# New opening orders, down-weight units moved to tiles 7, 8, 9 and 11, and 16 unread TensorE products

## The reference, cut to what matters

```python
xn = layernorm(x)                          # over the last axis
# FFN: NF4 weights, 4-bit codes with one absmax per 64 elements
Wg, Wu, Wd = dequant_nf4(gate), dequant_nf4(up), dequant_nf4(down)   # (1792,512) (1792,512) (512,1792)
ffn = (silu(xn @ Wg.T) * (xn @ Wu.T)) @ Wd.T
# S4: a 512-tap kernel K from the state matrices, a causal convolution along the last axis
s4 = irfft(rfft(xn, 1024) * rfft(K, 1024))[..., :512] + D * xn
```

## Time and profile before

| what | value |
|---|---|
| median of the runs | 471.67 us |
| the profiled execution's own time | 471.57 us |
| its span, first to last instruction | 469.7 us |
| PE (TensorE matmul) busy | 440.0 us |
| DVE busy | 396.7 us |
| ACT busy | 280.8 us |
| POOL busy | 209.1 us |
| mean granted TensorE clock | 0.993 |

### The profile page before, as it was taken

The page is one execution under the profiler, slowest core; times in us unless marked ns, Lnnn a source line. Parts: engine busy times, 40 slices in busy tenths (PEclk is TensorE's granted clock), DMA queues, the critical chain, the costliest instruction groups (busy, mean ns, idle before and its releaser), DMA issues.

```text
span 469.7 us, 7270 instructions
## 1 busy us (share of the span) xinstructions
PE 440.0 (94%) x2556; PEld 250.5 (53%) x2556; DVE 396.7 (84%) x629; ACT 280.8 (60%) x472; POOL 209.1 (45%) x180
## 2 busy tenths in 40 slices
PE   0789799999898699999999999999999999999997
PEld 0554344444343244444444444456544688888886
DVE  5966877988997979898897777969999799999993
ACT  7748737576787595687776767956232543545340
POOL 2672597364858685466655655957400000000000
PEclk9999999999999799999999999999999999999999
DMA  8461547111322454242512243347694021001101
GB/s 290 118 232 69 99 93 164 43 50 64 126 89 68 166 200 138 66 158 68 181 45 67 56 104 90 89 138 248 192 342 157 1 91 45 25 22 46 46 30 62
DMA packets 34168, 51.41 MB, mean 109 GB/s; under 512 B 13076, under 2 KB 14164, under 8 KB 33364
## 3 DMA queue, kind: packets, MB, share of 16 engines
q1 hardware_dynamic: 34132, 50.95, 35.1%
HBM read 38.03 MB, written 10.81 MB: 104 GB/s over the span
## 4 chain that ended last, share of the span: by engine, by line
PE 66%; DVE 12%; POOL 9%; issue 7%; ACT 4%; DMA 1%; SPq 0%; POOLq 0%; DVEq 0%; ACTq 0%
PE bank L2290 29%; PE bank L2417 21%; PE bank L2367 8%; PE bank L2357 6%; POOL work L885 3%; PE bank L2134 3%; ACT work L977 2%; POOL w L898 2%; DVE work L1350 1%; DVE h L1424 1%; DMA h<-in_x 1%; DVE work L1354 1%; DVE h L1539 1%; DVE h L1440 1%; POOL wd L898 1%
## 5 line engine op out<-in xcount | busy, mean ns | idle before, releaser
L977 ACT ACTIVATE work<-work 128x512 f32<-128x512 f32 (+1 forms) x234 | 130.2, 623 | 17.4 <-POOL work L885 11.4
L885 POOL TENSOR_SCALAR work<-work 128x512 f32<-128x512 int32 x39 | 85.1, 2182 | 69.5 <-DVE work L1350 56.6
L2290 PE MATMUL bank<-h 128*128 128x512 f16 x360 | 81.6, 379 | 0.5 <-DVE h L1411 0.4
L2134 PE MATMUL bank<-xT,w 128*128 128x512 f16 (+1 forms) x312 | 67.2, 374 | 4.4 <-DVE xT L1591 2.5
L2290 PEld LDWEIGHTS bank<-h 128*128 128x128 f16 x360 | 34.9, 98 | 43.8 <-issue 1.2
L2417 PE MATMUL bank<-wd,work 128*128 128x256 f16 x504 | 56.2, 273 | 0.0
L2290 PE MATMUL bank<-xT,w 128*128 128x512 f16 x240 | 55.4, 379 | 0.0
L2417 PEld LDWEIGHTS bank<-wd,work 128*128 128x128 f16 (+1 forms) x504 | 49.3, 98 | 6.0
L2134 PEld LDWEIGHTS bank<-xT,w 128*128 128x128 f16 x312 | 31.4, 101 | 37.5 <-DVE w L1364 3.1
L898 POOL TENSOR_SCALAR w<-work,sc 128x512 f16<-128x512 f32 x21 | 40.3, 1921 | 21.9 <-DVE work L1354 21.3
L1290 ACT ACTIVATE work<-h 128x896 f16<-128x896 f32 x30 | 27.9, 942 | 28.5 <-DVE h L2042 18.3
(11 more groups left out here) (196 smaller groups left out, 661.9 us busy)
## 6 DMA issues: line engine op xcount, KB each, us to landing
moved<-h SPq DMA_DIRECT2D x6, 1024.0 KB, 5.1
h<-moved SPq DMA_DIRECT2D x4, 1536.0 KB, 15.3
h<-in_x SPq DMA_DIRECT2D x8, 512.0 KB, 4.6
xT<-in_x SPq DMA_DIRECT2D x16, 256.0 KB, 3.6
out<-xT SPq DMA_DIRECT2D x15, 256.0 KB, 2.1
work<-in_q_gate SPq DMA_DIRECT2D x14, 256.0 KB, 2.8
work<-in_q_up SPq DMA_DIRECT2D x14, 256.0 KB, 3.1
work<-in_am_gate SPq DMA_DIRECT2D x28, 128.0 KB, 3.0
```

The lines of the kernel that those rows point to most:

```text
L885: pool.tensor_scalar(chain_room(u, "r"), qs[:, u % 2, :], RIGHT_FROM, RIGHT_FROM, ALU.max, ALU.subtract).then_inc(first_done, 1)
L977: nc.scalar.activation(room, qs[:, u % 2, :] if j == 0 else room, KNEE, scale=scale, bias=bias, alpha=below).then_inc(knee_done, 1)
L2134: mm = nc.tensor.matmul(out_b, weights(k)[:, unit, wl, f, :], xT[:, TPC * c + first:TPC * c + last, xl, f, :], start=(i == 0), stop=(i == ...
L2290: mm = nc.tensor.matmul(out_b, weight(wl, f), token(xl, f), start=(n == 0 and i in (1, 5)), stop=(n == 5), skip_group_check=i not in (1, 5))
```

## The change

- `EARLY_IN` goes from tiles 5, 6, 9, 12 to tiles 7, 8, 9, 11: the four down units that are made early stand between the up and the gate unit of these tiles.
- PE: ten products of the identity's bits (128x256 f16, into bank 1, unread) before the first transpose group, six more behind the fourth; `turn(7)` moves ahead of the up product of n = 1, which is no longer cut in two.
- POOL: `rstd(3)` (17 instructions) is removed; `first_pass` 4, 7 and 8 move ahead of the norms that they followed.
- DVE: `rstd(3)` in twelve steps is added; the whole list of the opening is reordered, with units 7 and 8 made before and among the token sums; the four `token_whole` of side 1 move from tile 3 into the opening. In `items` the order is WHOLE, SCALED with the unit's own `up_sums`, `weight_lo(u - 1)`; WHOLE waits for `wlo_done >= u - 2`.
- ACT: the opening is reordered; `chain(7)` and `chain(8)` come before the silus that they followed.
- SP: the absmax load of place 8 goes ahead of two small loads and of the DMA transposes of groups 12 to 15.

```diff
@@ -119,7 +119,7 @@
 
 
 
-EARLY_IN = (5, 6, 9, 12)
+EARLY_IN = (7, 8, 9, 11)
 EARLY = len(EARLY_IN)
 SEQ = list(range(9))
 for k in range(3, NM - 1):
...
@@ -490,7 +490,6 @@
         mv_done = sem("mv_done")
         acc_done = sem("acc_done")
         rs_step = sem("rs_step")
-        rs_next = sem("rs_next")
         xn_done = sem("xn_done")
...
         TURNED = 8
-        RSTD, RSTD_NEXT = 12, 17
+        RSTD = 12
...
                 turn(t)
             absmax_of(7)
             codes_of(8)
+            absmax_of(8)
             sp.dma_start(lstep, log_step.to_broadcast([P, 1])).then_inc(step_ld, 16)
             sp.dma_start(d_col, d_skip.to_broadcast([P, 1])).then_inc(d_ld, 16)
...
             for place in range(8, UNITS - 3):
                 codes_of(place + 1)
-                absmax_of(place)
+                if place > 8:
+                    absmax_of(place)
...
@@ -739,51 +740,10 @@
             pool.affine_select(out=ident[:], in_=ident[:], compare_op=ALU.not_equal, fill=1.0, base=0,
                                pattern=[[-1, P]], channel_multiplier=1).then_inc(id_done, 1)
 
-            def rstd(c):
-
...
                 c = t // TPC
-                if c < 3:
-                    pool.wait_ge(rs_step, RSTD * (c + 1))
-                else:
-                    pool.wait_ge(rs_next, RSTD_NEXT)
+                pool.wait_ge(rs_step, RSTD * (c + 1))
...
@@ -911,22 +871,21 @@
                 norm(t)
             first_pass(2)
             first_pass(3)
+            first_pass(4)
             for t in range(TPC, 2 * TPC):
                 norm(t)
-            first_pass(4)
             first_pass(5)
             for i in range(14):
                 v_step(i)
             first_pass(6)
             for t in range(2 * TPC, 3 * TPC):
                 norm(t)
-            rstd(3)
+            first_pass(7)
             for t in range(3 * TPC, NT):
                 norm(t)
-            first_pass(7)
+            first_pass(8)
             for i in range(EXP_STEPS):
                 exp_step(i)
-            first_pass(8)
...
@@ -1141,59 +1100,60 @@
             chain(1, 0, 5)
             norm(0)
             chain(1, 5, 6)
-            chain(2, 0, 1)
             x_hi(0)
             weight_hi(0)
             x_hi(1)
-            chain(2, 1, 2)
+            chain(2, 0, 1)
             x_hi(2)
             x_hi(3)
+            chain(2, 1, 2)
             weight_hi(1)
             chain(2, 2, 6)
             chain(3, 0, 2)
             weight_hi(2)
-            chain(3, 2, 6)
+            chain(3, 2, 4)
             x_hi(4)
+            chain(3, 4, 6)
+            silu(0)
+            chain(4, 0, 1)
+            weight_hi(3)
             x_hi(5)
-            weight_hi(3)
+            x_hi(6)
             act.wait_ge(b_mm, 1)
             nc.scalar.activation(yv[:, 0:2], bank[3][:, 0:2], ACT.Copy).then_inc(b_cp, 1)
-            x_hi(6)
             x_hi(7)
-            chain(4, 0, 3)
-            silu(0)
-            chain(4, 3, 6)
-            chain(5, 0, 3)
+            chain(4, 1, 6)
             h_hi(0)
             silu(1)
             weight_hi(4)
-            chain(5, 3, 6)
+            chain(5, 0, 6)
             h_hi(1)
+            silu(2)
             x_hi(8)
             weight_hi(5)
             x_hi(9)
             x_hi(10)
             x_hi(11)
-            silu(2)
+            silu(3)
             chain(6, 0, 6)
-            silu(3)
             silu(4)
             h_hi(4)
+            silu(5)
+            chain(7, 0, 6)
             x_hi(12)
             x_hi(13)
             x_hi(14)
             x_hi(15)
-            chain(7, 0, 6)
-            silu(5)
             silu(6)
+            chain(8, 0, 6)
             silu(7)
             silu(8)
             silu(9)
-            items(ACT_AT[7], ACT_AT[7] + 3)
+            weight_hi(6)
+            gate_copy(6)
             token_hi(0, 0)
             token_hi(0, 2)
             silu(10)
-            items(ACT_AT[7] + 3, ACT_AT[8])
             token_hi(0, 1)
             token_hi(0, 3)
...
-                    if u >= 2:
-
-                        dve.wait_ge(wlo_done, u - 1 if u < 4 or u in CHAINED else u)
+                    if u >= 3:
+                        dve.wait_ge(wlo_done, u - 2)
...
                     if u in CHAINED:
-                        i = (3, 2, 4)[i]
+                        i = (3, 4, 2)[i]
                     if i != 2:
                         step(u, i if i < 2 else i - 1)
                     elif u > 0:
                         weight_lo(u - 1)
-                        before = SEQ[u - 1]
-                        if before < GU and before % 2 == 1 and before // 2 in BLOCKED:
-                            up_sums(before // 2, u - 1)
+                    if i == 4 and SEQ[u] < GU and SEQ[u] % 2 == 1:
+                        up_sums(SEQ[u] // 2, u)
...
                     dve.wait_ge(xt_ld[c - 2], 16 * TPC)
+                elif s == 1 and i == 2:
+                    dve.wait_ge(xp_done, NT - POOL_NORMS)
                 elif s == 1 and i == 0:
-                    dve.wait_ge(xlo_done, NT)
+                    dve.wait_ge(xt_ld[1], 16 * TPC)
...
             step(0, SCALED)
+            step(1, WHOLE)
+            scales(7)
+            scales(8)
+            x_lo(0)
+            weight_lo(0)
+            x_lo(1)
+            step(1, SCALED)
+            x_lo(2)
+            x_lo(3)
+            weight_lo(1)
             stats(5)
             stats(6)
-            scales(7)
             stats(7)
-            scales(8)
             moments(4, 8)
-            step(1, WHOLE)
             rstd(1, 0)
             rstd(1, 1)
             rstd(1, 2)
-            x_lo(0)
+            scales(9)
             rstd(1, 3)
-            weight_lo(0)
             rstd(1, 4)
-            x_lo(1)
             rstd(1, 5)
-            step(1, SCALED)
+            step(2, WHOLE)
             rstd(1, 6)
             rstd(1, 7)
-            x_lo(2)
             rstd(1, 8)
-            x_lo(3)
+            step(2, SCALED)
             rstd(1, 9)
             rstd(1, 10)
-            weight_lo(1)
             rstd(1, 11)
-            scales(9)
-            step(2, WHOLE)
-            scales(10)
-            step(2, SCALED)
-            scales(11)
             weight_lo(2)
             stats(8)
+            x_lo(4)
+            scales(10)
             step(3, WHOLE)
+            scales(11)
+            step(3, SCALED)
+            h_mul(0)
             scales(12)
-            step(3, SCALED)
-            x_lo(4)
+            weight_lo(3)
             x_lo(5)
-            weight_lo(3)
+            x_lo(6)
             stats(9)
-            x_lo(6)
             x_lo(7)
...
             rstd(2, 2)
-            h_lo(0)
+            step(4, WHOLE)
             rstd(2, 3)
-            step(4, WHOLE)
             rstd(2, 4)
             rstd(2, 5)
             step(4, SCALED)
             rstd(2, 6)
             rstd(2, 7)
             rstd(2, 8)
-            h_mul(1)
+            h_lo(0)
...
             rstd(2, 11)
+            h_mul(1)
             weight_lo(4)
+            step(5, WHOLE)
+            step(5, SCALED)
             h_lo(1)
-            step(5, WHOLE)
+            stats(12)
             x_lo(8)
-            step(5, SCALED)
...
-            stats(12)
+            stats(13)
             weight_lo(5)
             x_lo(9)
-            stats(13)
             x_lo(10)
+            x_lo(11)
+            h_mul(2)
             stats(14)
-            x_lo(11)
             stats(15)
             moments(12, 16)
-            h_mul(2)
+            rstd(3, 0)
+            rstd(3, 1)
+            rstd(3, 2)
             h_mul(3)
+            rstd(3, 3)
+            rstd(3, 4)
+            rstd(3, 5)
             step(6, WHOLE)
+            rstd(3, 6)
+            rstd(3, 7)
+            rstd(3, 8)
             step(6, SCALED)
+            rstd(3, 9)
+            rstd(3, 10)
+            rstd(3, 11)
+            token_whole(0, 1)
             h_mul(4)
-            token_whole(0, 1)
+            token_whole(0, 3)
             h_lo(4)
-            token_whole(0, 3)
+            h_mul(5)
+            step(7, WHOLE)
+            step(7, SCALED)
             for t in range(12, 16):
                 x_lo(t)
-            h_mul(5)
             h_mul(6)
-            items(DVE_AT[7], DVE_AT[7] + 1)
+            step(8, WHOLE)
+            step(8, SCALED)
+            token_whole(1, 2)
+            token_whole(1, 3)
             h_mul(7)
-            h_mul(8)
             token_whole(0, 0)
             token_whole(0, 2)
             token_sum(0, 0)
+            h_mul(8)
             token_sum(0, 1)
+            token_sum(0, 2)
+            token_whole(1, 0)
             h_mul(9)
-            items(DVE_AT[7] + 1, DVE_AT[8])
-            token_sum(0, 2)
             token_sum(0, 3)
+            weight_lo(6)
             token_lo(0, 0)
             token_lo(0, 2)
+            token_whole(1, 1)
             h_mul(10)
             token_lo(0, 1)
```

(21 more changed lines are left out.)

36 lines of the change are left out of this document (removed).

## The result

| what | before | after |
|---|---|---|
| median, runs taken together | 471.75 us (4 runs, 471.19 to 472.29) | 459.08 us (4 runs, 458.88 to 460.08) |
| the profiled execution's own time | 471.57 us | 460.08 us |
| its span | 469.7 us | 458.3 us |
| mean granted TensorE clock in it | 0.993 | 0.996 |

The ratio is 0.9736, 95% interval 0.9717 to 0.9754: 2.6% faster. The forecast was 459.5 us, in a range of 456.5 to 467.0.

The account below looks back on a forecast made before the run. PE was taken to bound the kernel (busy 94% of the span), with 19.0 us of waits and clock loss to gain. 471.57 - 2.4 - 2.6 - 1.9 - 7.45 + 1.4 = 458.6, plus 0.9: 459.5 us, range 456.5 to 467.

Parts of the forecast that it names:

- tiles 3 to 5: PE's waits of 1.74 and 0.45 us for DVE go, a new 0.3 comes in tile 4: gain 1.9 us.
- stop in tile 5, with clock: Moving tile 5's down unit removes PE's 5.40 us stop and 2.05 of clock loss: gain 7.45 us, lower bound 2.1.
- tiles 7 and 8: Third unit and new `items` order put 2.0 us ahead of tile 8's `join(1, 8, 0)`: loss 1.4; tile 7, 0.
- allowance: 0.9 us added to the time for joints left with less than a us of room.
- Opening, start of the products: `x_lo(1)` ends near 16.5, six unread products follow, first product begins at 17.7: 1.5 us earlier, bounds 0 and 2.7.
- Opening, clock: Products from 16.4 without a gap bring full clock between 20.5 and 21.5: gain 0.9 us, bounds 0 and 2.5.
- rival (c): Opening: unread products do nothing for the clock, 0.9 us of gain goes, 460.4 us; forecast with (c) 0.68.
- Opening, the wait for the norm: `rstd(1)` ends about 24.6; PE reaches `turn(4)` near 25.1 and waits some 0.7 us for the norm.
- Rival (e): POOL holds up tile 8's added DVE steps by one pass each: loss 7.3, time 464.5 us; chance 0.02.
- (a): Other engines do not get ahead in the opening; only tile 5's stop goes: 465.5 us; chance 0.21.
- (b): The stop moves to tiles 7, 8 and 9 instead of going: 479.6 us, slower; chance 0.05.
- (d): Nothing moves: PE's stops reappear one for one, 471.6 us; chance 0.04.

Follow-up runs that it names:

- number 11: The changed kernel once more, unchanged, in the group of number 12: 459.65 us, ratio 0.9723.
- numbers 3 and 12: The changed kernel without the 16 unread products, run in two groups: 460.05 us (ratio 0.9743) and 460.54 us (ratio 0.9748).
- number 1: The kernel before with only the tiles of the early down units changed, to 7, 8, 9, 11: 467.27 us, ratio 0.9904.
- number 4: The changed kernel with `first_pass(4)` on POOL behind the norms of groups 4 to 7 again: 458.65 us, ratio 0.9713.
- number 8: The kernel before with the 16 unread products added at the same two places: 471.62 us, ratio 0.9984.
- number 7: The changed kernel with the old order inside the units (WHOLE, `weight_lo` with `up_sums`, SCALED) in tiles 3 to 13, opening new: 461.48 us, ratio 0.9764.
- number 2: The changed kernel with the early down units back at tiles 5, 6, 9, 12, new orders and products kept: 461.06 us, ratio 0.9771.
- number 6: The changed kernel with the early down units at tiles 6, 7, 9, 11, one in tile 6 in place of tile 8: 459.55 us, ratio 0.9732.
- 5: The changed kernel with `first_pass(4)` behind the norms and without the 16 unread products: 460.19 us, ratio 0.9739.
- 9: The changed kernel with `first_pass(4)` behind the norms, tile 8's `inverse_e` behind both joins, and the old unit order for places 9 and 10 only: 457.45 us, ratio 0.9679.
- 10: The changed kernel with tile 8's `inverse_e` steps moved behind both joins: 458.97 us, ratio 0.9707.

## Why the prediction was right, and where it was not

The forecast was right in its time and in most of its places. Term by term, predicted and measured in the profiled execution:

| step | predicted | measured |
|---|---|---|
| opening, tiles 0 and 1 | 2.4 | 1.06 |
| opening, tile 2 | 2.6 | 2.76 |
| tiles 3 to 5 | 1.9 | 1.68 |
| stop in tile 5, with clock | 7.45 | 7.61 |
| tiles 7 and 8 | -1.4 | -2.72 |
| tiles 9 to 13 | 0 | 1.11 |
| allowance | -0.9 | |
| sum | 12.1 | 11.5 |

That the sum came so near is in part luck: the opening gave 1.3 us less than forecast and tiles 7 and 8 cost 1.3 more, and a gain of 1.1 in tiles 9 to 13 that the forecast did not have and the allowance of 0.9 made up for most of it.

**Opening, start of the products.** Near: `x_lo(1)` ends at 16.98 (16.30 + 0.68) for 16.5, and the first product comes at 17.13 for 17.7. In this execution transposes and unread products ran at the full rate, so that the six cost nothing and PE waits 0.62 behind them. In number 11 they ran at half the rate as forecast, and the first product came at 17.70.

**Opening, clock.** The gain was under-rated and then misplaced. The clock was full before the first product in the execution of after (the upper bound, 2.5 us, for the 0.9 taken), and at 17.82, just behind it, in number 11. The reason given is not borne out: numbers 3 and 12 have no products and the full clock at 18.34 and 17.27 all the same, and number 1, with PE's program of before, had it for a time from 16.58 on. The mechanism of rival (c) fits better, though not its price, since the clock's gain comes without the products too. What the products bring, if it is real, is some 0.9 us; that the clock falls less often later is a guess.

**Opening, the wait for the norm.** This is the step that failed: "PE reaches `turn(4)` near 25.1 and waits some 0.7 us for the norm." It waited 2.90. PE came to it at 23.4, earlier because the products began 0.6 us sooner and no clock was lost (1.4 to 1.9 forecast), and the norm at 26.3, later than forecast, since `rstd(1)` ended at 25.4 for 24.6. Those 0.8 us are what the `first_pass(4)` beside it costs `rstd(1)`: it takes 3.71 us from first step to last, and 2.90 in number 4, where the pass stands behind. PE was taken 1.7 us too late and the norm 0.5 too early; the two errors add to the 2.2 between 0.7 and 2.90. The clock then fell behind the wait, which the forecast did not have at all: 1.7 us. So a larger clock gain became a smaller gain of the stage, 1.06 us for 2.4 (1.3 counted from PE's first instruction, and 2.0 in number 11, where the clock held). The sign "granted clock 1.00 from about 21 us to the end" failed with it. "PE goes on near 31.6" was 33.01 in that execution, and 32.10 where the clock held. "The `first_pass(4)` put ahead of the norms is covered" looked at POOL's idle time alone. The pass starts only when its codes land, at 22.20, beside `rstd(1)`, and what it delays is DVE.

**Tile 2.** Right to 0.2 us, and numbers 1 and 8 show the old wait of 2.6 wherever the old list stands.

**Tiles 3 to 5.** The 1.74 and the 0.45 went as predicted. The new wait for the low half of tile 4's up unit was seen and mis-sized: 1.07 for 0.3. Number 7, without it, shows that it comes from `weight_lo(u - 1)` standing last.

**The stop in tile 5.** Right in size, wrong in ownership. "That unit costs DVE two steps and a low half... With it gone, DVE has the join ready": number 1, which only moves the unit, leaves 1.24 us, and number 2, which leaves the unit there, only 2.16. The stop had two waits of DVE for POOL ahead of it, 1.87 and 1.47 us; moving the unit takes away the second, the order inside a unit the first. The forecast saw the second alone. The lower bound of 2.1 was far too low, since number 1 took 6.2 us; it left out that without a long stop no clock is lost.

**Tiles 7 and 8.** Tile 7 costs 0.4 us by its starts, for 0. Tile 8 costs 2.3 for 1.4 (the forecast's own terms give 1.3: 2.0 less 0.5 caught up and 0.2 left), and by other means. The wait on DVE is 1.03, and 1.44 in number 11; number 6 shows that with the new order it does not need the third unit. The forecast booked the new order of `items` as a loss of 0.75 us, the `up_sums` ahead of the join. Number 7 shows the opposite: with the old order tile 7 waits 1.31, tile 8 1.41 and tile 11 0.74, and the time is 1.8 to 2.4 us longer. The other wait of tile 8, 0.95, was not forecast: an ACT step on the bank behind `h_mul(n)`, which DVE reaches later. Rival (e) did not come. Two inverse steps from 194.81 take 0.74 for both beside a POOL pass of 2.67 us. In number 11 the same two take 1.16 beside a pass of 2.25 and PE's wait for the join is longer by as much: here 0.42 us goes to the one engine or the other. The 1.16 us of the earlier trace rows, which the forecast took for free of delay, had, by this measure, 0.4 of delay in them. A WHOLE step at 189.68 took 1.09 where others take 0.68, with a POOL cast of 1.06 us beside it: 0.4 us, not a whole pass. By the Trainium skill ("SBUF — State Buffer", "SBUF: two separate sides") the inverse steps, which read two operands from SBUF, would have stood for the pass; this trace does not agree with it there.

**The other rivals.** (a): number 1 is its case, the unit gone and no lead, and took 467.27 us for its 465.5; with the new opening the waits of the opening and of tile 4 that it kept are gone, as number 7 shows. (b) and (d): no PE wait from tile 6 to the end is over 1.1 us in the profile after.

**Left open:** why tiles 6 and 7 wait for ACT in number 6 and tile 7 does not in the kernel after; why the short waits of tile 13 in the kernel before, most of the 1.1 us gained in tiles 9 to 13, are gone; how much of the 0.9 us of the products is real, and how much of number 4's 0.8 us on DVE reaches the time.

## What to carry to other kernels

A stop can have more than one cure, each enough for most of it. Before booking it to one edit, ask what each other edit does to the same wait, and test the parts one at a time: here 1.0% and 2.3% made 2.6%. When a forecast makes the bottleneck engine arrive earlier at a joint and a supplier later, compute the margin at both ends of their ranges, because a gain ahead of the joint turns into a wait at it. An engine's idle time is not free to fill if the work put there slows another engine's steps: the pass in POOL's idle time cost DVE 0.8 us on the path that PE waited for. The order of the steps inside one unit decided the waits of the steady tiles; the lead gained in the opening did not last to tile 5.

## What the runs showed of the hardware

The granted clock is not the same from run to run of one program. PE's instructions up to the first products are the same in the kernel before and in number 1, and the clock was full (2.4 GHz) by 24.27 in one, from 16.58 in the other with a fall to 1.2 GHz from 20.00 to 23.41. The kernel after has it from 13.64 in one execution and from 17.82 in the other. Behind the wait for the norm it fell in the execution of after (2.90 us of wait) and in numbers 3 (2.84), 7 (2.83), 12 (2.72), 2 (2.39), 5 (2.09), 9 (2.08) and 4 (1.65), and did not in numbers 10 (2.70), 11 (2.37) and 6 (2.19): the length of the wait alone does not tell. It did not fall behind 2.16 us in tile 5 of number 2, and did behind the 5.40 of the earlier trace rows and of number 8. Behind tile 2's wait it fell in number 8 (2.60) and did not in the kernel before (2.59). The transposes of 128x128 f32 ran at the full rate when the clock was up: twelve in 1.97 us against 2.82.

DVE and POOL slow each other by parts of a step. Beside a POOL pass of 1.92 us two DVE steps of 128x4 took 0.60 and 0.53 us, 0.16 without it (number 4). Two DVE steps of 128x256 with two operands each took 0.74 us in one execution of the kernel after and 1.16 in the other, and the POOL pass beside them 2.67 and 2.25.
